# Sixteen matrix products of ones on TensorE at the head of the first attention of an eight-stage block

## The reference

```python
def _L0_xattn_ref(qk, v, masks, Wq, bq, Wk, bk, Wv, bv, Wo, bo):      # W = 128, H = 8, D = 128, DK = 64
    qp, vp, mp = _to_patches(qk), _to_patches(v), _to_patches(masks)  # 8 batches x 4 patches of 128 x 128
    q = jnp.einsum('ed,bdw->bew', Wq, qp) + bq[:, None]
    k = jnp.einsum('ed,bdw->bew', Wk, qp) + bk[:, None]
    val = jnp.einsum('ed,bdw->bew', Wv, vp) + bv[:, None]
    scores = jnp.einsum('bhdi,bhdj->bhij', qh, kh) / jnp.sqrt(jnp.asarray(dh, qh.dtype))   # 8 heads of dh = 8
    scores = jnp.where(mp[:, :, None, :] > 0, scores, jnp.asarray(-1000000000.0, scores.dtype))
    attn = jax.nn.softmax(scores, axis=-1)
    o = jnp.einsum('bhij,bhdj->bhdi', attn, vh).reshape(BN, DK, W)
    o = jax.nn.gelu(o, approximate=False)
    out = jnp.einsum('de,bew->bdw', Wo, o) + bo[:, None]
...
x = x + _L0_xattn_ref(_layernorm(x, axis=-1), ctx_4096, mask_Bx1x4096_ff1, ...)   # the stage of the change
x = x + _L0_ffn_ref(_layernorm(x, axis=-1), ...)
x = x + _L1_xattn_ref(_layernorm(x, axis=-1), ctx_4096, ...)     # takes the top 76 of 128 context channels
x = x + _L1_ffn_ref(_layernorm(x, axis=-1), ...)
x = x + _L2_xattn_ref(_layernorm(x, axis=-1), ctx_4096, ctx_4096, ...)
x = x + _L2_ffn_ref(_layernorm(x, axis=-1), ...)
x = x + _L3_xattn_ref(_layernorm(x, axis=-1), ctx_4096, ctx_4096, pos_BxS2, mask_BxSxS2_ik0, ...)
x = x + _L3_ffn_ref(_layernorm(x, axis=-1), ...)
return x
```

## Time and profile before

| | |
|---|---|
| median of 3 runs | 1654.74 us (1654.24 to 1656.63) |
| profiled execution | 1655.96 us, of which the span from the first to the last instruction is 1654.2 us |
| PE busy | 1477.4 us, 89% of the span |
| PEld (weight loads) | 1055.1 us, 64% |
| DVE busy | 981.1 us, 59% |
| ACT busy | 547.8 us, 33% |
| POOL busy | 531.9 us, 32% |
| mean granted TensorE clock | 0.974 |
| chain that ended last | PE 70%, DVE 12%, issue 5%, POOL 4%, SP's queue 4%, DMA 3%, ACT 2% |

### The profile page before, as it was taken

One profiled execution on the slowest core, in us unless ns is written; L12 is line 12 of the kernel. 1 busy time (PEld: TensorE's weight loads), 2 busy tenths in 40 slices (PEclk: granted clock), 3 DMA queues, 4 the chain that ended last, 5 costly groups with the idle time before them and its releaser, 6 DMA issues.

```text
span 1654.2 us, 20269 instructions
## 1 busy us (share of the span) xinstructions
PE 1477.4 (89%) x6854; PEld 1055.1 (64%) x6854; DVE 981.1 (59%) x2158; ACT 547.8 (33%) x1414; POOL 531.9 (32%) x531
## 2 busy tenths in 40 slices
PE   0788888877888989999899998899999999999898
PEld 0344444434766677676678776777777777777555
DVE  2565666655768334888322245677777777777543
ACT  1223222233342213454323113334434334434332
POOL 4100000004523232341312113545545545443163
PEclk9999999999999979999899999999999999999799
DMA  5111111112313210010111104111111111110001
GB/s 157 53 39 37 33 32 33 28 36 90 96 58 102 64 51 1 8 33 1 39 39 51 39 1 147 32 58 51 46 58 51 46 58 51 46 48 4 7 1 51
DMA packets 63481, 77.52 MB, mean 47 GB/s; under 512 B 7138, under 2 KB 34018, under 8 KB 63252
## 3 DMA queue, kind: packets, MB, share of 16 engines
q1 hardware_dynamic: 62416, 74.99, 14.9%
q10 hardware_dynamic: 964, 1.25, 0.2%
HBM read 57.34 MB, written 10.49 MB: 41 GB/s over the span
## 4 chain that ended last, share of the span: by engine, by line
PE 70%; DVE 12%; issue 5%; POOL 4%; SPq 4%; DMA 3%; ACT 2%; POOLq 0%; DVEq 0%; ACTq 0%
PE bank L423 15%; PE bank L428 14%; PE bank L427 14%; SPq L910 3%; PE bank L2331 3%; PE bank L1961 2%; PE bank L2309 2%; PE bank L1950 2%; PE bank L2224 2%; DMA ring_l<-k 2%; PE bank L1959 2%; PE bank L2206 2%; PE bank L490 1%; DVE xn L1807 1%; PE bank L2318 1%
## 5 line engine op out<-in xcount | busy, mean ns | idle before, releaser
L1012 POOL TENSOR_TENSOR ring_l<-stage,ring_h 128x512 fp32r<-128x512 f32 x133 | 179.0, 1363 | 235.6 <-ACT ring_h L1168 235.6
L423 PE MATMUL bank<-xTh_b,ring_h 128*128 128x512 f32 x464 | 191.3, 412 | 2.8 <-issue 1.5
L427 PE MATMUL bank<-xTl_b,ring_h 128*128 128x512 f32 x464 | 185.4, 400 | 0.0
L428 PE MATMUL bank<-xTh_b,ring_l 128*128 128x512 f32 x464 | 185.2, 399 | 0.0
L1119 POOL TENSOR_TENSOR q<-xn 128x512 f32<-128x512 f32 x64 | 82.2, 1284 | 220.6 <-DVE xn L1807 220.6
L423 PE MATMUL bank<-ring_h,o3h 128*128 128x512 f32 x256 | 125.7, 491 | 0.8 <-issue 0.8
L1446 ACT ACTIVATE probs<-bank,nbias 128x128 f32<-128x128 f32 x256 | 90.5, 366 | 54.7 <-DVE nbias L1831 54.7
L1437 ACT ACTIVATE probsT<-bank 128x512 f32<-128x512 f32 x64 | 38.3, 598 | 205.6 <-PE bank L2318 205.6
L423 PEld LDWEIGHTS bank<-xTh_b,ring_h 128*128 128x128 f32 x464 | 88.8, 191 | 23.2 <-issue 4.4
L428 PEld LDWEIGHTS bank<-xTh_b,ring_l 128*128 128x128 f32 x464 | 88.5, 191 | 21.7
L428 PE MATMUL bank<-ring_h,o3l 128*128 128x512 f32 x256 | 101.0, 395 | 0.0
(11 more groups left out here) (327 smaller groups left out, 3535.0 us busy)
## 6 DMA issues: line engine op xcount, KB each, us to landing
stage<-in_units_dram SPq DMA_DIRECT2D x133, 256.0 KB, 3.2
ring_h<-q SPq DMA_DIRECT2D x64, 64.0 KB, 2.0
ring_l<-k SPq DMA_DIRECT2D x64, 64.0 KB, 2.1
raw_k<-kvs SPq DMA_DIRECT2D x16, 256.0 KB, 2.1
raw_v<-kvs SPq DMA_DIRECT2D x16, 256.0 KB, 2.0
kraw<-raw_k SPq DMA_DIRECT2D x16, 256.0 KB, 3.4
v<-raw_v SPq DMA_DIRECT2D x16, 256.0 KB, 3.0
stage<-in_context_dram SPq DMA_DIRECT2D x8, 256.0 KB, 3.1
```

The lines of the kernel that those rows point to most:

```text
L423: ins = nc.tensor.matmul(out_ap, wh, mh, start=start, stop=False)
L427: nc.tensor.matmul(out_ap, wh, ml, start=False, stop=False)
L428: return nc.tensor.matmul(out_ap, wl, mh, start=False, stop=stop)
L1012: nc.gpsimd.tensor_tensor(ring_l[:, place_of(u), :], stage[:, u % STAGE, :], f32(ring_h[:, place_of(u), :]), ALU.subtract).then_inc(w_lo, 1)
```

## The change

PE's program gets a helper `busy_pe(n)` that issues n products, each of a 128 x 128 piece of ones as weights with the 128 x 512 tile of ones. They write bank 3 and neither wait for nor signal anything. It is called once, with 16, in the pass `g = -1`, between the last scores product of group 0 and the transposition of its maxima.

```diff
--- before.py
+++ after.py
@@ -1996,6 +1996,12 @@
             keys0(0)
             values0(0)
             t.wait_ge(su_mk, 3)
+
+            def busy_pe(n):
+
+                for _ in range(n):
+                    nc.tensor.matmul(bank[3][:], ones_r[:, 0:P], ones_r[:, :], start=True, stop=True)
+
             for g in range(-1, G0):
                 for p in range(4):
                     if p == 0 and g + 2 < G0:
@@ -2016,6 +2022,8 @@
                         projection0((g + 3) // 2)
                 if g >= 0:
                     outputs0(g, 3)
+                if g < 0:
+                    busy_pe(16)
                 if g + 1 < G0:
                     turned_max0(g + 1)
             turned_outputs0(G0 - 1)
```

## The result

The changed kernel takes **1648.67 us** (median of 5 runs, 1647.57 to 1650.11) against 1654.74 for the kernel before (5 runs beside them, 1653.54 to 1656.63): a ratio of 0.9962, 95% interval 0.9949 to 0.9975, or 6 us less. The forecast was 1650.4. The profiled execution took 1647.57 us, its span is 1645.8.

The account below looks back on a forecast made before the run. The first attention was taken to be paced by PE at its lower clock level, with transfers between groups. Terms +2.2, -0.4, -4.5, -0.3 and -1.3 gave -4.3 us from 1654.74: 1650.4 us, range 1647.5 to 1652.5.

Parts of the forecast that it names:

- The row of sixteen: Sixteen products ahead of L1979, eleven at the lower clock level, partly hidden in 3.70 us of idle: +2.2 us.
- the bound of +1.0: Lower bound for the sixteen products' cost, if the clock rises after four: 4.9 us long, +1.0 us.
- L1979 to L1950: From the maxima's transposition to the first scores product, 2.37 us before; faster product spacing saves 0.4 us (0 to 0.7).
- the one and a half steps: Product spacings on the path between L1979 and L1950, each falling from 0.59 to 0.34 us: -0.4 us.
- The group's work: PE's work in the first group, first L1950 to last L1961, shrinks from 10.76 to 6.2 us: -4.5 us.
- The groups of the rivals: Further groups at the upper clock level take 13.8 us against 19.46, so -5.6 us each.
- The stay in the second group: The upper level lasts some 2 us into the second group before falling: -1.3 us (0 to -5.6).
- the transfer path: Query and key transfers after the last turned product, not VectorE, set the next group's start, 7.2 us behind it.
- holds for some groups more: Rival: the clock stays up two to seven groups more in the first attention, 1639 down to 1611 us; chance 0.20.
- holds throughout: Rival: the clock stays up for the whole first attention, fifteen groups at -5.6 us, about 1568 us; chance 0.04.
- Costs and gives nothing: Rival: no rise within the sixteen products, or a fall before L1950; the run ends +3.1 us, 1657.8 us; chance 0.08.

Follow-up runs that it names:

- sixteen again: The changed kernel itself, unaltered, run and profiled a second time beside the other row lengths on one chip; 1650.60 us, ratio 0.9959 to the kernel before.
- all fills: Changed kernel plus fourteen products of ones in every later pass, eight ahead of L1979 and six ahead of the first scores; 1589.93 us, ratio 0.9617.

## Why the prediction was right

Seen step by step, with 0.40 us taken off for the later start:

- **The row of sixteen, forecast +2.2 us.** Measured +0.8 (68.11 against 66.92 + 0.40): the rise came 2.2 us into the row, after about five products and not eleven. In the second execution that was profiled it was +2.4. The price is not one number, and the bound of +1.0 was not low enough.
- **L1979 to L1950, forecast -0.4.** Measured 1.47 us against 2.37: -0.9 (and 1.46 in the second execution). The products between the two shrank by more than the one and a half steps that the forecast counted.
- **The group's work, forecast -4.5.** Measured 6.22 us where 6.2 stood, -4.5, in each of three profiles (sixteen, sixteen again, eight). The groups of the rivals, which would hold the clock longer, were priced too high, though: the forecast took 19.46 us for each of the old ones, the longer first interval, where they last 19.0 on average, and 13.8 for the new ones, where 14.08 were measured with all fills. The transfers did bind the next group, as said: from the last L1961 to L1950 it is 7.17 us against 7.46, the difference being the shorter product: -0.3.
- Together 0.8 - 0.9 - 4.5 - 0.3 = **-4.9 us** at the second group, forecast -3.0.
- **The stay in the second group, forecast -1.3.** Nil. The clock fell at 79.3, behind the first pause (1.67 us, ahead of L1979), and the product at 79.36 took 0.76. In the second execution it held over that pause and fell at 82.3, 1.8 us behind it, with a wait of 0.62 us between, and ahead of the next pause; with eight it fell 1.5 us behind the first. The step that failed is "a further 2 us or so of the second group": it let the delay of 1.3 us of the earlier trace rows run from the end of the second pause, and the loss belongs to the first.
- So the errors cancelled, which was luck: the row and the way to L1950 gave 1.9 us more than forecast and the transfer path held, the stay gave 1.3 less, and it came to -4.9 by the second group where -4.3 stood. In the second execution, with the dearer row, it was -3.4.

The median moved by 6 us, and the profile by 8.4. Where is the rest? The last scores product of the stage came at 343.72 and now at 338.87, 5.2 us earlier once aligned; the remaining 3.6 us lie behind it, and the forecast has no term for them. Between the rise after the stage and the end of the low stretch near 600 us the same work took 221.9 us before and takes 218.5 now. Busy time by stretch, of the kernel before and then of the changed one:

```profile
398.20:620.10 221.90, 191.67 (x859) 150.28 (x858) 121.42 (x280) 72.04 (x223) 79.85 (x97) 0.91 0.23 74
620.10:1654.20 1034.10, 987.38 (x4938) 756.46 (x4936) 629.19 (x965) 368.79 (x1028) 410.89 (x379) 0.98 0.12 39
```
```profile
393.30:611.80 218.50, 188.06 (x855) 147.26 (x854) 120.64 (x280) 72.13 (x223) 79.82 (x97) 0.93 0.23 75
611.80:1645.80 1034.00, 987.34 (x4942) 756.27 (x4940) 629.28 (x966) 368.67 (x1028) 411.20 (x379) 0.98 0.12 39
```

The same VectorE work (121.42 and 120.64), the same end to 0.1 us, but a clock of 0.91 and 0.93: the low stretches between them fall elsewhere and are shorter in sum (30.7 us and not 41.0). From the last L1950 to the end it is 1310.5 us before, 1309.2 with four products, 1309.9 with thirty-two; 1306.9, 1308.6 and 1306.8 with sixteen, sixteen again and eight. So the three that gain all gain 2 to 4 us here as well, and four products, which moved nothing ahead of it, 1.3 us. Whether that belongs to a start some 5 us earlier or to chance, one profile of each kernel doesn't say, and it **stays open**.

Of the rivals, *holds for some groups more* and *holds throughout* didn't happen to this kernel, and the experiments say what they would have needed. By the table of the Trainium skill (TensorE: Matmul & The Clock Gate, "Why this matters for your kernels") the pauses of this stage would have been too short to lose the clock, and it would have stayed up. The measurement decides against it here: lost behind 1.67 us in the changed kernel, and with no pause at all at 106.0 with all fills. *Costs and gives nothing* is what four products (no rise) and thirty-two (rise, but too long a row) come to, 1.0013 and 1.0001.

## What to carry to other kernels

Where a stage is PE's and its products have the long form of the lower level, find the waits of PE in it and fill each with dense products that write a bank nobody reads: here one row at the head was worth 0.4%, and with fourteen products in every pass it was 3.8%. A row that fits into the wait, eight products here, does as much as a longer one. The clock once raised was kept for most of the stage only where both pauses of a pass were filled, and even then it fell now and then; one pause of the two left open gave alternation, and a longer row at the head gave nothing. And look at the durations, not at the clock row: that row read 9 for a stage that ran at half speed, because it held no record.

## What was not expected of the hardware

- The fall with PE busy for 3.40 of 3.40 us (102.6 to 106.0 with all fills), amid products of 64 columns and of few rows, and its absence at the same place in the runs with the same instructions, which fell later in the same manner. What the chip counts is not idle time alone. Whether the sparse products cause it stays open.
- The rise comes at a time that differs between executions of one kernel: 2.2 and 5.6 us into the same row in two of them. With eight products, lasting 3.52 us, it still came, at 66.6; the mean clock of all five timed runs was 0.880 to 0.883 (0.974 in the profiled execution of the kernel before), so in each of them.
- Products of ones alone raise the clock as real operands do.
